# Two-layer conditional MLP with attention pooling on one core: pooling exponentials moved into tile 10 of the first layer, and one shared ring of four PSUM banks

## The reference, cut to what matters

```python
# x: 16 batches of 512 tokens x 512 features
h = gelu(x @ fc1_w.T + fc1_b)                       # 2048 hidden
y = concat(h @ fc2_w.T + fc2_b,                     # 384 shared outputs
           h @ experts_w[i].T + experts_b[i])       # 128 outputs of the batch's expert
x = x + y
attn = tanh(x @ W1 + b1)                            # 128 wide
scores = attn @ v                                   # one per token
# mask per batch: prefix (l <= j), postfix (l >= j) or all but j
p = softmax(where(mask, scores, -1e30))
x = x + (p @ x) / count(mask)
```

## Time and profile before

| | |
|---|---|
| median of three runs | 1475.81 us |
| the profiled execution | 1475.46 us |
| its span in the trace | 1473.4 us |
| TensorE matmul, busy | 1416.4 us, 96%, 6488 instructions |
| VectorE, busy | 1196.0 us, 81%, 1749 instructions |
| ScalarE, busy | 677.0 us, 46%, 888 instructions |
| DMA | 59.25 MB, mean 40 GB/s |
| mean granted TensorE clock | 0.995 |

### The profile page before, as it was taken

One profiled execution on the slowest core, in us unless ns is written; L12 is line 12 of the kernel. 1 busy time (PEld: TensorE's weight loads), 2 busy tenths in 40 slices (PEclk: granted clock), 3 DMA queues, 4 the chain that ended last, 5 costly groups with the idle time before them and its releaser, 6 DMA issues.

```text
span 1473.4 us, 16247 instructions
## 1 busy us (share of the span) xinstructions
PE 1416.4 (96%) x6488; PEld 655.4 (44%) x6488; DVE 1196.0 (81%) x1749; ACT 677.0 (46%) x888; POOL 0.2 (0%) x4
## 2 busy tenths in 40 slices
PE   6999999999999999999999999999999999999996
PEld 2444444444444444444444444444444444444444
DVE  6866877969778797877979778797877979778796
ACT  4736355262643626345262643626345362643612
POOL 0000000000000000000000000000000000000000
PEclk9999999999999999999999999999999999999998
DMA  5220020100202011020110202011020110200000
GB/s 208 76 88 16 8 79 1 54 33 15 72 2 84 1 44 42 8 79 0 50 37 15 72 1 87 1 38 49 8 79 1 50 36 15 73 0 29 1 22 36
DMA packets 27148, 59.25 MB, mean 40 GB/s; under 512 B 5698, under 2 KB 6082, under 8 KB 24642
## 3 DMA queue, kind: packets, MB, share of 16 engines
q1 hardware_dynamic: 26642, 57.70, 11.3%
q10 hardware_dynamic: 432, 0.53, 0.1%
HBM read 41.45 MB, written 16.78 MB: 40 GB/s over the span
## 4 chain that ended last, share of the span: by engine, by line
PE 72%; DVE 19%; ACT 8%; issue 0%; DVEq 0%
PE pf L269 44%; PE po L314 23%; DVE raw L139 7%; DVE raw L370 5%; DVE raw L420 3%; PE pa L345 3%; ACT raw L403 3%; ACT L403 1%; ACT hh L148 1%; PE psc L355 1%; DVE xr L139 1%; ACT g L293 1%; DVE x2l L139 1%; DVE raw L142 0%; DVE mx L189 0%
## 5 line engine op out<-in xcount | busy, mean ns | idle before, releaser
L269 PE MATMUL pf<-xh,w1h 128*128 128x512 f16 x1024 | 389.5, 380 | 3.1 <-ACT xh L148 2.1
L269 PE MATMUL pf<-xh,w1l 128*128 128x512 f16 x1024 | 389.0, 380 | 0.4 <-DVE w1l L145 0.4
L269 PE MATMUL pf<-xl,w1h 128*128 128x512 f16 x1024 | 389.2, 380 | 0.1
L314 PE MATMUL po<-hh,w2l 128*128 128x512 f16 x768 | 291.8, 380 | 0.0
L314 PE MATMUL po<-hh,w2h 128*128 128x512 f16 x768 | 291.6, 380 | 0.0
L314 PE MATMUL po<-hl,w2h 128*128 128x512 f16 x768 | 291.6, 380 | 0.0
L145 DVE SCALAR_TENSOR_TENSOR hl<-g,ix,hh 128x512 f16<-128x512 f32 x240 | 179.4, 748 | 127.2 <-ACT hh L148 126.7
L293 ACT ACTIVATE g<-pf,b1s,ds 128x512 f32<-128x512 f32 x240 | 186.7, 778 | 202.7 <-PE pf L269 201.5
L370 DVE TENSOR_TENSOR_SCAN raw<-raw 128x512 f32<-128x512 f32 x180 | 213.1, 1212 | 56.2 <-ACT raw L403 56.2
L139 DVE TENSOR_TENSOR raw<-raw 128x512 f32<-128x512 f32 (+1 forms) x315 | 202.8, 683 | 1.1
L148 ACT ACTIVATE hh<-g,ix 128x512 f16<-128x512 f32 x240 | 173.1, 721 | 7.3
(11 more groups left out here) (121 smaller groups left out, 1181.2 us busy)
## 6 DMA issues: line engine op xcount, KB each, us to landing
er<-in_ew SPq DMA_DIRECT2D x16, 1024.0 KB, 4.9
out<-xr SPq DMA_DIRECT2D x64, 256.0 KB, 2.3
xr<-in_xT SPq DMA_DIRECT2D x62, 256.0 KB, 4.3
raw<-in_w SPq DMA_DIRECT2D x16, 256.0 KB, 6.8
er<-in_w SPq DMA_DIRECT2D x3, 1024.0 KB, 10.3
xr<-in_xT ACTq DMA_DIRECT2D x2, 256.0 KB, 5.1
raw<-in_aw SPq DMA_DIRECT2D x1, 256.0 KB, 4.9
ebs<-in_eb SPq DMA_DIRECT2D x16, 0.5 KB, 2.2
```

Source lines behind the costliest of these rows:

```text
L269: return e.matmul(bank[:, :], w[:, k, c, :], x[:, c, :], start=c == 0 and i == 0, stop=c == KD - 1 and i == 2)
L314: m = e.matmul(bank[:, :], w, h[:, k, :], start=k == 0 and i == 0, stop=k == NH - 1 and i == 2)
```

## The change

The pooling's exponentials go from behind tile 15 to tile 10 of the first layer: at `k == 10`, after `low(b, 9)` and in the last batch `see`, the rest of `pool_rows` is drawn, `exps` is put on ScalarE's list (behind `gelu(b, 10)` and `high(b, 10)`), and `pool_rest` becomes the generator that `fill` draws from. `psc` is gone and `pf` has a fourth bank. Banks are handed out in turn by `turn()`, to the tiles, to the score, and to the last batch's transposes, and each user waits for whatever emptied the bank last.

```diff
-    pf = [nc.alloc_psum_tensor(f"pf{i}", [P, S], f32) for i in range(3)]
+    pf = [nc.alloc_psum_tensor(f"pf{i}", [P, S], f32) for i in range(4)]
-    psc = nc.alloc_psum_tensor("psc", [P, S], f32)
...
+    turns, emptied = [0], [None] * 4
+
+    def turn():
+
+        n = turns[0] % 4
+        turns[0] += 1
+        return n, (() if emptied[n] is None else (emptied[n],))
...
+    bank_of = {}
+
     def fc1(b, k, cs=range(KD)):
-        n = b * NH + k
-        bank = pf[n % 3]
-        free = (g_done[n - 3],) if n >= 3 else ()
+        if 0 in cs:
+            bank_of[b, k] = turn()
+        n, free = bank_of[b, k]
...
     def gelu(b, k):
-        n = b * NH + k
+        n, bank = b * NH + k, bank_of[b, k][0]
...
+        emptied[bank] = g_done[n]
...
     def score(b):
-        free = (scored[b - 1],) if b else ()
-        score_done[b] = PE.op(lambda e: e.matmul(psc[:, :], avs[:, :], att, start=True, stop=True), tanh_done[b], av_ready, *free)
-        scored[b] = AC.op(copy(sc, psc[:, :]), score_done[b], *((s_free[b - 1],) if b else ()))
+        n, free = turn()
+        score_done[b] = PE.op(lambda e: e.matmul(pf[n][:, :], avs[:, :], att, start=True, stop=True), tanh_done[b], av_ready, *free)
+        emptied[n] = scored[b] = AC.op(copy(sc, pf[n][:, :]), score_done[b], *((s_free[b - 1],) if b else ()))
...
     def natural_up(b, c):
 
-        free = g_done[b * NH + NH - 1] if c < 3 else nat_ready[0]
+        n, free = turn()
...
-    def natural_low(b, c, high):
+    def natural_low(b, c, up):
+        n, high = up
...
-        nat_ready[c] = DV.op(tt(l3, pf[c % 3][:, :].rearrange("p (a b) -> p a b", a=4), n3.bitcast(f32), ALU.subtract), high)
+        emptied[n] = nat_ready[c] = DV.op(tt(l3, pf[n][:, :].rearrange("p (a b) -> p a b", a=4), n3.bitcast(f32), ALU.subtract), high)
...
             if last and 10 <= k < 14:
                 see(b, k - 10)
+            if k == 10:
+                finish()
+                exps(b - 1)
+                pools[0] = pool_rest(b - 1)
             fill(0.0 if k in (13, 14) else 1.1 if 6 <= k < 10 else 1.85)
         if b:
             low(b, NH - 1)
-            finish()
-            exps(b - 1)
-            pools[0] = pool_rest(b - 1)
```

More of the change, by code:

```diff
@@ L261, in build @@
     fc1_done, fc2_done, g_done, hh_done, h_ready, evac, x2_ready = {}, {}, {}, {}, {}, {}, {}
+    bank_of = {}
     def fc1(b, k, cs=range(KD)):
-        n = b * NH + k
-        bank = pf[n % 3]
-        free = (g_done[n - 3],) if n >= 3 else ()
+        if 0 in cs:
+            bank_of[b, k] = turn()
+        n, free = bank_of[b, k]
         def product(e, w, x, c, i):
-            return e.matmul(bank[:, :], w[:, k, c, :], x[:, c, :], start=c == 0 and i == 0, stop=c == KD - 1 and i == 2)
+            return e.matmul(pf[n][:, :], w[:, k, c, :], x[:, c, :], start=c == 0 and i == 0, stop=c == KD - 1 and i == 2)
         three = ((w1h, xh), (w1h, xl), (w1l, xh))
@@ L290, in gelu @@
     def gelu(b, k):
-        n = b * NH + k
+        n, bank = b * NH + k, bank_of[b, k][0]
         free = (h_ready[n - GR],) if n >= NH + GR else ()
-        g_done[n] = AC.op(lambda e: e.activation(g_of(b, k), pf[n % 3][:, :], ACT.Gelu, bias=b1s[:, k:k + 1],
+        g_done[n] = AC.op(lambda e: e.activation(g_of(b, k), pf[bank][:, :], ACT.Gelu, bias=b1s[:, k:k + 1],
                                                  scale=ds1[:, b % 2, k:k + 1]), fc1_done[b, k], ds1_ready[b, k], b1_ready, *free)
+        emptied[bank] = g_done[n]
     def high(b, k):
@@ L483, in natural_up @@
     def natural_up(b, c):
-        free = g_done[b * NH + NH - 1] if c < 3 else nat_ready[0]
+        n, free = turn()
         def fn(e):
             for t in range(4):
-                m = e.matmul(pf[c % 3][:, t * P:(t + 1) * P], xr[:, b % XB, c, t * P:(t + 1) * P], eye[:, :], start=True, stop=True)
+                m = e.matmul(pf[n][:, t * P:(t + 1) * P], xr[:, b % XB, c, t * P:(t + 1) * P], eye[:, :], start=True, stop=True)
             return m
-        done = PE.op(fn, free, eye_ready, x2_ready[b, c])
+        done = PE.op(fn, *free, eye_ready, x2_ready[b, c])
         n3 = nh[:, :, c * P:(c + 1) * P]
-        return AC.op(lambda e: e.activation(n3, pf[c % 3][:, :].rearrange("p (a b) -> p a b", a=4), ACT.Copy), done, fc1_done[b, NH - 1])
-    def natural_low(b, c, high):
+        return n, AC.op(lambda e: e.activation(n3, pf[n][:, :].rearrange("p (a b) -> p a b", a=4), ACT.Copy), done, fc1_done[b, NH - 1])
+    def natural_low(b, c, up):
+        n, high = up
         n3, l3 = (t[:, :, c * P:(c + 1) * P] for t in (nh, nl))
-        nat_ready[c] = DV.op(tt(l3, pf[c % 3][:, :].rearrange("p (a b) -> p a b", a=4), n3.bitcast(f32), ALU.subtract), high)
+        emptied[n] = nat_ready[c] = DV.op(tt(l3, pf[n][:, :].rearrange("p (a b) -> p a b", a=4), n3.bitcast(f32), ALU.subtract), high)
     def pool_last(b):
```

## The result

The changed kernel takes 1547.66 us (median of 4 runs, 1546.99 to 1548.48) against 1475.63: ratio 1.0487, 95% interval [1.0469, 1.0505]. It is 72 us slower. 1537 was forecast, with 1514 to 1550 as the range and 1529 to 1547 for the forecast's own mechanism; the time lies in the first and 0.7 us above the second.

A forecast was written before the change was run, and what follows sets the result against it. VectorE's list between the exponentials' end and split_x2_low was taken to bound each batch. 14 x 2.94 = 41.2, last batch 3.3 and clock 16.8 gave +61.3 us on 1475.8: 1537 us, range 1514 to 1550.

The forecast's parts named there:

- the forecast's own mechanism: Later split_x2_low and a slower TensorE clock behind attend(b, 0) lengthen batches: 1529 to 1547 us, chance 0.62.
- Where the exponentials end, and the table load: ScalarE behind tile 10: exponentials end at 673.93, VectorE goes on 12.97 us earlier; a table load takes 1.28 us.
- VectorE's list behind them: Ahead of split_x2_low(b, 0): 26 pooling operations in place of 16, plus first-layer leftovers; 2.94 us later per batch.
- The wait for `low` of tile 15: TensorE waits some 1.1 us in block 0, the reciprocal being drawn first; not added, inside the wait at attend.
- The evacuation of block 0: On ScalarE behind the four xh copies: ends about 0.9 us before VectorE comes to the residual, so no cost.
- Banks and ring: Four banks shared by tiles and score, with ScalarE's pause behind tile 10: costed at nothing.
- The clock: TensorE drops to 1.2 GHz behind the 3.5 us idle at attend(b, 0): bounds 0 and 1.92 us a batch.
- 14 x 1.2 = 16.8: Slow TensorE time behind attend(b, 0): 1.2 us in each of 14 batches, 16.8 us in all.
- stays down longer: Slow TensorE clock lasts twice as long behind the idle, 3.8 us a batch: 1574 us, chance 0.06.
- The last batch: Ahead of its first residual 25 operations in place of 15, the transpose about 3.6 us later; together +3.3 us.
- the 0.3 us that I had credited to the end: Near the kernel's end pool_rest is through earlier, worth 0.3 us.
- The rival of the faster kernel: At attend(b, 0): with 19 or fewer pooling operations ahead of split_x2_low TensorE never waits; 1448 us, chance 0.05.

The follow-up runs named there:

- without the draws: The changed kernel, exponentials still at tile 10, but nothing drawn from pool_rest before the second layer: 1455.76 us, ratio 0.9868 to the kernel before.
- the ring alone: The changed kernel's shared ring of four banks, with the exponentials back behind tile 15: 1475.0 us against 1475.38 for the kernel before, ratio 1.0.
- the move alone: The kernel before with the exponentials moved to tile 10, keeping three tile banks and the score's own bank: 1548.94 us, ratio 1.05.

## Why the prediction was right, point by point

- **Where the exponentials end, and the table load:** as walked, 6.07 us against 6.04.
- **VectorE's list behind them:** 31.40 us against 31.53. The count of 26 operations from the credits holds. Its price, 2.94 us a batch, is confirmed by the batch of 91.44 us at full clock; with the last batch 44.5 us were put, and 45.2 stayed with the clock held up (1520.6 - 1475.38), about 44 by the traces. That the loss comes from this list was shown three ways: without the draws it turned into a gain of 20 us, with two operations fewer ahead a batch became 1.5 us shorter, and with the exponentials early and the rest in its old place the kernel won 32.
- **The wait for `low` of tile 15:** 1.07 us against 1.1, inside the later wait. The idle at `attend` was 3.32 against 3.5. Of the 0.2 us between, the walk of the list explains less than half (91.44 against 91.51 a batch); the rest is that TensorE came 1.24 us later than before, and not the 1.07 of its wait.
- **The evacuation of block 0:** the cover was 0.88 us against 0.9. The difference is written there the wrong way round (12.97 - 8.81 - 6.9 is -2.7), but read rightly as 2.7 us later; it was 2.60.
- **Banks and ring:** nothing by themselves, shown by the ring alone and by the move alone.
- **The clock:** right in kind, too small in size. The term "14 x 1.2 = 16.8" is the step that was mis-sized; it measured 27.1 us by the times and 28.4 by the traces, 2.0 a batch, beyond the bound of 1.92, and this makes nearly all of the 10.7 us between forecast and result. My reason for going below the bound was that part of the low stretch falls into the idle. It does in 8 of the 14 batches, but only 0.3 to 1.1 us of it, and in 5 of these 8 the stretch is twice as long (827.6 to 834.4 at 0.50 in one of them, against 643.3 to 646.7). A batch with the long one loses 2.7 to 3.0 us (94.19 to 94.45, less 91.44), the others 1.4 to 1.7. In each case that is, to 0.2 us, half of the low time that falls on work: 3.4 / 2 = 1.7 for a short stretch that lies wholly behind the idle, measured 1.6 to 1.7. The rival "stays down longer", with 0.06, was true of a third of the batches, though at 3.0 us at most and not 3.8.
- **Luck in it:** that the clock falls in all 14 batches didn't follow from the reason given, an idle longer than the single one of 2.39 us that had cost. Idles of 2.46 and 3.06 are longer too, and with them the clock held in 7 and in 5 of the 14. The kernel in which it fell in 7 took 1530.58 us, and the one in which it fell behind none of these idles 1520.6.
- **The last batch:** its idle went from 2.39 to 4.36 us. In the kernel with eight extra matmuls, where the clock stays up through batches 1 to 14, the transpose stands here:

```profile
1454.63 2.05 PE L507 MATMUL pf<-eye,xr 128*128 128x128 f32 x8 [4.36 <-DVE xr L147]
```

It starts 1454.63 - 1364.46 = 90.17 us after `attend(14, 0)`, against 1409.95 - 1323.30 = 86.65 before: 3.5 us later, 3.6 in the walk. From the transpose to the end of the span it is 63.5 us in the kernel before and 63.4 in the change, so the 0.3 us that I had credited to the end did not come.

The rival of the faster kernel had the right point of decision, the place in VectorE's list, but its condition of 19 operations or fewer holds only for a list that starts right behind the exponentials. The kernel without draws has 16 ahead of `split_x2_low` and still waits 0.51 us, since its list starts 11.8 us behind them. The change draws too much, and the same early exponentials with two operations drawn save 32 us.

## What to carry to other kernels

Starting a stage earlier gains only if what is queued between its start and the next late waiter doesn't grow. Here an engine with 19% of idle time lost some 44 us, because a credit that counts planned time, and not who is free, put ten operations ahead of the one that TensorE waited for, and the early exponentials put the first layer's leftovers there too. Count the operations that stand ahead of the critical one, in list order, before and after; fill only known standstills, and leave the rest where it was.

## What the runs showed that I had not expected

- How often TensorE's clock falls to the 1.2 GHz level behind one idle in each of 14 batches: idles of 1.59 and 1.70 us never, of 2.46 in 7, of 3.06 in 9, of 3.32 in all 14. It is no matter of the idle's length alone, since one of 2.29 us in batch 0, the same in all ten kernels, made it fall in three. Nor is the price fixed: in the change a low stretch lasted 3.4 us in 9 batches and 6.8 us in 5, and cost 1.4 to 3.0 us.
- Eight useless matmuls in each of 14 batches made the kernel 27 us faster.
- A wait costs TensorE more than its length: 1.95 us for 1.70 and 0.77 for 0.51 at `attend`, 0.63 for 0.45 at tile 14. The first matmuls behind it take 0.97 us on the chain in place of 0.70.
